# A recurrent attention stage with its output rows by transposes, an earlier first decay part, gate strips on GpSimd and VectorE, and a third decay part masked after the exponential

## The reference, cut to what matters

```
log_D  = (cs[s] - cs[t] + ig[t])  for t <= s, else -inf      # per sequence and head, 256 x 256
D_mat  = exp(log_D - max_t log_D)
C      = (q @ k.T / sqrt(32)) * D_mat
C_norm = C / (max(|sum_t C|, exp(-max_log_D)) + eps)
h      = layernorm(C_norm @ v) * (1 + ln_w)                  # over a head's 32 features
y      = (a * sigmoid(g)) @ w2[e] + b2[e]                    # expert e of the token
out    = x + h * silu(y)
```

## Time and profile before

| | |
|---|---|
| median of 3 runs | 233.12 us (232.3 to 234.32) |
| the profiled execution | 232.86 us, of it 231.0 us span |
| PE busy | 211.4 us, 92% |
| DVE busy | 173.7 us, 75% |
| ACT busy | 135.4 us, 59% |
| POOL busy | 107.5 us, 47% |

### The profile page before, as it was taken

One profiled execution on the slowest core, in us unless ns is written; L12 is line 12 of the kernel. 1 busy time (PEld: TensorE's weight loads), 2 busy tenths in 40 slices (PEclk: granted clock), 3 DMA queues, 4 the chain that ended last, 5 costly groups with the idle time before them and its releaser, 6 DMA issues.

```text
span 231.0 us, 6117 instructions
## 1 busy us (share of the span) xinstructions
PE 211.4 (92%) x1847; PEld 173.8 (75%) x1856; DVE 173.7 (75%) x490; ACT 135.4 (59%) x309; POOL 107.5 (47%) x140
## 2 busy tenths in 40 slices
PE   7998989889999999999999999999999999999430
PEld 6887745546555555699999999999999999986110
DVE  5998699975776767587679888988798878570590
ACT  2388757897887977655555555556556555520220
POOL 7667920077777771003333354336443643474250
PEclk9999999999999999999999999999999999999995
DMA  6999999998111115110790211220211000000993
GB/s 166 326 396 414 310 254 249 250 256 223 52 60 49 57 55 127 31 25 25 211 271 14 61 26 54 54 70 6 66 45 34 25 14 29 23 23 14 297 315 103
DMA packets 29761, 29.32 MB, mean 127 GB/s; under 512 B 3319, under 2 KB 24831, under 8 KB 29729
## 3 DMA queue, kind: packets, MB, share of 16 engines
q1 hardware_dynamic: 25138, 20.46, 28.9%
q0 software_dynamic: 3424, 8.38, 14.7%
q10 hardware_dynamic: 1168, 0.10, 0.4%
HBM read 20.01 MB, written 9.38 MB: 127 GB/s over the span
## 4 chain that ended last, share of the span: by engine, by line
PE 74%; DVE 10%; issue 5%; DMA 4%; ACT 1%; POOL 1%; SPq 1%; DVEq 0%; POOLq 0%; ACTq 0%
PE bank L1213 15%; PE head_bank L1213 15%; PE bank L1222 14%; PE head_bank L1169 6%; PE bank L1181 5%; PE bank L1156 5%; PE bank L1198 4%; PE bank L1155 3%; DVE stats L703 3%; PE bank L1095 2%; DMA xw<-y_tokens 2%; PE head_bank L1136 2%; DMA x_sb<-in_L_attn_x 1%; PE head_bank L1064 1%; DVE mv L709 1%
## 5 line engine op out<-in xcount | busy, mean ns | idle before, releaser
L458 POOL DMA_INDIRECT y_tokens<-ffn,idx x39 | 39.4, 1010 | 74.7 <-DVE ffn L1002 74.1
L452 POOL DMA_INDIRECT xs_sorted<-xw,pos x32 | 31.2, 975 | 25.8 <-DVE pos L849 16.4
L1222 PE MATMUL bank<-w_sb,dm 128*128 x312 | 41.3, 275 | 0.5 <-DVE dm L986 0.5
L1213 PE MATMUL bank<-xsT,wc 128*128 128x128 f32 x320 | 39.5, 276 | 0.3 <-DVE wc L869 0.3
L1222 PEld LDWEIGHTS bank<-w_sb,dm 128*128 128x128 f32 x312 | 38.0, 192 | 0.7 <-issue 0.7
L1213 PEld LDWEIGHTS bank<-xsT,wc 128*128 128x128 f32 x320 | 37.5, 192 | 0.7 <-DVE wc L869 0.5
L1213 PE MATMUL head_bank<-xsT,wc 128*128 128x128 f32 x304 | 37.0, 275 | 0.0
L877 DVE TENSOR_TENSOR cm<-dm,head_bank 128x1024 f32<-128x1024 f32 (+1 forms) x32 | 29.1, 950 | 9.6 <-PE head_bank L1169 6.5
L1213 PEld LDWEIGHTS head_bank<-xsT,wc 128*128 128x128 f32 x304 | 35.4, 192 | 0.0
L605 ACT ACTIVATE wc<-w_sb 128x512 f32 x39 | 24.6, 630 | 15.1 <-issue 15.0
L591 ACT ACTIVATE dm<-bank 128x512 f32<-128x512 f32 x48 | 26.9, 595 | 5.9 <-PE bank L1156 4.9
(11 more groups left out here) (199 smaller groups left out, 360.2 us busy)
## 6 DMA issues: line engine op xcount, KB each, us to landing
x_sb<-in_L_attn_x SPq DMA_DIRECT2D x16, 256.0 KB, 5.0
w_sb<-in_L_ffn_w SPq DMA_DIRECT2D x8, 512.0 KB, 8.3
w_sb<-negated_rows POOLq DMA_DIRECT2D x8, 508.0 KB
xs_sb<-xs_sorted SPq DMA_DIRECT2D x13, 193.5 KB, 2.6
xs_sorted<-b_sb SPq DMA_DIRECT2D x1, 2048.0 KB, 13.0
xw<-y_tokens SPq DMA_DIRECT2D x8, 256.0 KB, 4.8
out_x<-xw SPq DMA_DIRECT2D x8, 256.0 KB, 3.4
y_tokens<-ffn,idx POOLq DMA_INDIRECT x39, 2.3
```

Source lines behind the costliest of these rows:

```text
L452: pool.indirect_dma_start(xs_dram, bass.IndirectOffsetOnAxis(ap=pos[:, t:t + 1], axis=0), xw[:, t, :], None).then_inc(s_scat, 16)
L458: pool.indirect_dma_start(y_dram, bass.IndirectOffsetOnAxis(ap=idx[:, j:j + 1], axis=0), ys_sb[:, j // CH % 2, j % CH, :], None, bounds_ch ...
L1213: last = pe.matmul(bank[2 * (j % 2) + k][:, c * P:(c + 1) * P], wc[:, j % 3, m:m + P], xsT[:, j % 2, :], start=True, stop=True)
L1222: last = pe.matmul(bank[6 + j % 2][:, 0:D], uT[:, j % 2, c, :], w2_sb[:, bass.ds(e * (HC * D) + c * D, D)], start=(c == 0), stop=(c == HC ...
```

## The change

1. **Token rows.** `token_rows` uses two transposes in place of the two matmuls with `spread`. The ones move to column 0 of each head in `u_all`, the 31 values to columns 1 to 31; column 32 gets the sum of the 31, by a new reduction `last_columns` on VectorE for two sequences at once (turns b = 3, 5, ..., 15, and once after the loop). It is the last feature with the wrong sign, and `gamma` is negated there. `outputs` goes from VectorE to ScalarE, 256 columns.
2. **First decay part earlier.** TensorE: `scores(b+1)`, `log_decay(b+2, 0)`, `values_sum(b)`, `log_decay(b+2, 1)`, `log_decay(b+2, 2)`, `token_rows(b)`. ScalarE: `decay(b+2, 0)`, `evac_u(b)`, `decay(b+2, 1)`, `decay(b+2, 2)`, `outputs(b)`.
3. **Strips.** The twelve right strips of j = 1 to 3 are made by GpSimd, one after the other, after its weight DMAs and before the indirect DMAs. `left_rows` goes to VectorE, in turn b for b+3.
4. **Third part.** `log_decay(b, 2)` has no mask matmul. After the exponential, `masked(b)` on VectorE takes the minimum of `dm` part 2 and `keep` (3e38 or 0), 128 x 512, in place; it runs in turn b-1 after `weigh(b-1)`, for b = 0 between the two parts of `weigh(0)`.

```diff
@@ gpsimd
-            pool.tensor_copy(spread[:, :, 0:DH - 1], idh[:, :, 0:DH - 1]).then_inc(s_spread, 1)
...
+            pool.memset(keep[:, :], BIG).then_inc(s_keep, 1)
...
+            pool.affine_select(out=keep[:, :], in_=keep[:, :], compare_op=ALU.is_ge, fill=0.0,
+                               base=0, pattern=[[1, P]], channel_multiplier=-1).then_inc(s_keep, 1)
...
+            pool.tensor_scalar(last_of_head, last_of_head, -1.0, None, ALU.mult).then_inc(s_gamma, 1)
...
+            pool.wait_ge(s_ind, 4)
+            pool.wait_ge(s_sel, 2)
+            pool.wait_ge(s_seld, 1)
+            for j in range(1, NBS):
+                for h in range(NH):
+                    pool.tensor_scalar(right[:, h, j, :], sel[:, j, :], rmask[:, 0, h:h + 1], rmask[:, 1, h:h + 1],
+                                       ALU.mult, ALU.add).then_inc(s_rtp, 1)
@@ scalar
-            def left_rows(b):
...
+            def outputs(b):
+                act.wait_ge(s_o, b + 1)
...
+                act.activation(u_all[:, 2 * b:2 * b + 2, :, 0:DH],
+                               bank[7][:, 0:2 * D].rearrange("p (k h d) -> p k h d", k=2, h=NH), ACT.Copy).then_inc(s_oe, 1)
...
             for b in range(2):
                 for m in range(3):
                     decay(b, m)
-                left_rows(2 + b)
             for b in range(B):
                 if b == B - 1:
                     act.wait_ge(s_cm, 2 * (B - 1))
                     gate(0)
+                if b + 2 < B:
+                    decay(b + 2, 0)
                 evac_u(b)
                 if b + 2 < B:
-                    for m in range(3):
-                        decay(b + 2, m)
+                    decay(b + 2, 1)
+                    decay(b + 2, 2)
+                outputs(b)
...
-                    right_rows(b // 4 + 1, 2 * (b % 4))
-                    right_rows(b // 4 + 1, 2 * (b % 4) + 1)
-                if b + 4 < B:
-                    left_rows(b + 4)
@@ vector
+            def masked(b):
+                dve.wait_ge(s_keep, 2)
+                dve.wait_ge(s_dm, 3 * b + 3)
+                tail = dm[:, b % 2, :, 2, :]
+                dve.tensor_tensor(tail, tail, keep[:, :].unsqueeze(1).to_broadcast([P, NH, P]), ALU.min).then_inc(s_mk, 1)
...
+            def last_columns(b):
+                dve.wait_ge(s_oe, b + 2)
+                rows = u_all[:, 2 * b:2 * b + 4, :, :]
+                dve.tensor_reduce(rows[:, :, :, DH], rows[:, :, :, 1:DH], AX.X, ALU.add).then_inc(s_lc, 1)
...
+                left_rows(2)
                 for b in range(B):
                     weigh(b)
                     if b == 0:
                         evac_q(NQA + 1)
-                    if b >= 1:
-                        outputs(b - 1)
+                    if b == 0:
+                        dve.wait_ge(s_sel, 2)
+                        dve.wait_ge(s_seld, 1)
+                    if b + 1 < B:
+                        masked(b + 1)
+                    if b + 3 < B:
+                        left_rows(b + 3)
+                    if b >= 3 and b % 2:
+                        last_columns(b - 3)
@@ tensor
-                if m != 1:
+                if m == 0:
                     pe.matmul(bank[n % 2][:, :], ident_bf[:, :], maskn[:, :, :].rearrange("p h t -> p (h t)"), start=True, stop=False)
...
-                    last = pe.matmul(bank[7][:, k * n:(k + 1) * n], uTs[:, k * P:(k + 1) * P],
-                                     spread[:, :, :].rearrange("p h d -> p (h d)"), start=True, stop=True)
+                    last = pe.transpose(bank[7][:, k * P:(k + 1) * P], uTs[:, k * P:(k + 1) * P], ident[:, :])
...
+                if b + 2 < B:
+                    log_decay(b + 2, 0)
                 values_sum(b)
                 if b + 2 < B:
-                    log_decay(b + 2, 0)
                     log_decay(b + 2, 1)
+                    log_decay(b + 2, 2)
...
                 token_rows(b)
-                if b + 2 < B:
-                    log_decay(b + 2, 2)
```

More of the change, by code:

```diff
@@ L101, in mlstm_moe_block @@
         center = sb("center", [P, NH, DH])
-        spread = sb("spread", [P, NH, DA])
         triones = sb("triones", [P, S])
         maskn = sb("maskn", [P, NH, P], BF16)
+        keep = sb("keep", [P, P])
         desc8 = sb("desc8", [P, E])
@@ L300, in mlstm_moe_block @@
         s_maskc = sem("s_maskc")
-        s_spread = sem("s_spread")
+        s_lc = sem("s_lc")
+        s_keep = sem("s_keep")
+        s_mk = sem("s_mk")
+        s_rtp = sem("s_rtp")
         s_uones = sem("s_uones")
@@ L875, in weigh, with left_rows @@
                 for m0, m1 in ((0, 2), (2, 3)):
-                    dve.wait_ge(s_dm, 3 * b + m1)
+                    if m1 == 2:
+                        dve.wait_ge(s_dm, 3 * b + m1)
+                    else:
+                        if b == 0:
+                            masked(0)
+                        dve.wait_ge(s_mk, b + 1)
                     dve.tensor_tensor(cm[:, b % 2, :, m0:m1, :], dm[:, b % 2, :, m0:m1, :],
                                       head_bank[:, :, m0 * P:m1 * P].rearrange("p h (m t) -> p h m t", t=P), ALU.mult).then_inc(s_cm, 1)
-            def outputs(b):
-                dve.wait_ge(s_o, b + 1)
-                if b == FORGET:
-                    dve.tensor_copy(tm[:, :, :], bank[7][:, 3 * P:3 * P + 2 * R].rearrange("p (k r) -> p k r", k=2)).then_inc(s_tm, 1)
-                dve.tensor_copy(u_all[:, 2 * b:2 * b + 2, :, :].rearrange("p k h d -> p (k h d)"),
-                                bank[7][:, 0:2 * NH * DA]).then_inc(s_oe, 1)
+            def left_rows(b):
+                if b >= 4:
+                    dve.wait_ge(s_ld, 3 * (b - 3))
+                dve.tensor_scalar(left[:, b % 4, :], sel[:, b // 4, :], lmask[:, 0, b % 4:b % 4 + 1],
+                                  lmask[:, 1, b % 4:b % 4 + 1], ALU.mult, ALU.add).then_inc(s_lf, 1)
+            def last_columns(b):
+                dve.wait_ge(s_oe, b + 2)
+                rows = u_all[:, 2 * b:2 * b + 4, :, :]
+                dve.tensor_reduce(rows[:, :, :, DH], rows[:, :, :, 1:DH], AX.X, ALU.add).then_inc(s_lc, 1)
             def attention():
@@ L909, in attention @@
                 product(0)
-                outputs(B - 1)
+                last_columns(B - 2)
             def normalise(g):
@@ L1152, in log_decay @@
                         pe.wait_ge(s_lf, b - 1)
[L1153 to L1154 removed]
+                    if j == 0:
+                        pe.wait_ge(s_rt, 2)
+                    else:
+                        pe.wait_ge(s_rtp, NH * j)
+                if m == 0:
                     pe.matmul(bank[n % 2][:, :], ident_bf[:, :], maskn[:, :, :].rearrange("p h t -> p (h t)"), start=True, stop=False)
                 pe.matmul(bank[n % 2][:, :], left[:, b % 4, s0:s0 + P], right[:, :, j, t0:t0 + P],
[L1157 removed]
+                          start=(m != 0), stop=True).then_inc(s_ld, 1)
             def scores(b):
```

39 lines of the change are left out of this document (15 added, 24 removed).

## The result

The changed kernel takes **240.31 us** (median; 239.9 to 242.23) where the kernel before took 232.75 beside it: ratio 1.0322, interval 1.0274 to 1.037. It is slower by 7.6 us; forecast were 240.5 us and 7.4 more. All that follows is read in the profiled execution of 239.9 us, whose span is 238.0, 7.0 over that of before.

The account below looks back on a forecast made before the run. TensorE looked like the bound before; after the change VectorE would decide the loop. Start 3.8, loop 2.6 and end 1.0 sum to 7.4 us on 232.86, 240.3, stated as 240.5; range 234.8 to 244.

Parts of the forecast that it names:

- The loop, +2.6: Eleven turns from scores(4) to scores(15), set by VectorE: 41.7 us against 39.1 before, 2.6 us slower.
- the rules: Loop: earliest starts of VectorE's minimum, `weigh` and the next scores in each turn; 7.4 to 7.6 us per pair of turns.
- The rival in which TensorE goes on deciding: Loop: turns of 3.1 us if the minimum costs 0.3 and not 0.6; total 230.0 us, chance 0.08.
- TensorE's turn, 3.1: Loop: TensorE's own work and waits in one turn sum to 3.1 us; alone, a gain of 0.4 us a turn.
- The start, +3.8: Up to scores(4): 56.7 us against 52.9, about 2.7 from the VectorE-GpSimd conflict and 1.1 from VectorE's longer queue.
- the conflict, priced at 2.7: Start: VectorE's small routing instructions each wait for one GpSimd strip, both reading SBUF; about 2.7 us.
- the rival without a conflict, at 0.22: Start: GpSimd's strips run beside VectorE's routing instructions; scores(4) only 1.1 us later, total 237.8 us, chance 0.22.
- The worse start: Start: strips of 0.75 us or more and TensorE falling to half clock; total 243 to 244 us, chance 0.12.
- The end, +1.0: Loop's end: ScalarE's outputs 14 and 15 each put about 0.5 us before an expert block; 1.0 us slower.
- The total, 240.5: Whole kernel: 7.4 us more than the profiled 232.86 is 240.3; stated as 240.5 us, with chance 0.45.
- It cancels: Whole kernel: loop turns of 3.35 us pay for the slower start; about 232.8 us, chance 0.13.
- The scatters: Indirect DMAs start at about 52 instead of 46.6 us, yet stay hidden behind the loop with 2 us to spare.

Follow-up runs that it names:

- its second profile: The changed kernel run again with nothing changed, beside the kernel before at 233.47 us: 241.3 us, ratio 1.0328.
- the kernel with three mends: Changed kernel with third part masked on TensorE, GpSimd's strips behind the six routing instructions, sorted rows copied before the last two outputs: 232.43 us, ratio 0.9977.
- the fastest one: The kernel with three mends, plus all positions in VectorE's turn 0 and eight of GpSimd's twelve strips moved to VectorE: 227.92 us, ratio 0.9786.

## Why the prediction was right, point by point

**The loop, +2.6: measured +2.5.** Both the rule and its pattern hold: 3.14 and about 4.5 us by turns, 7.64 for the pair quoted above where the rules gave 7.4 to 7.6, because the minimum, which waits for the third exponential, begins at S + 3.81 (79.34 less 75.53) and not S + 3.65. VectorE's work of 0.6 + 0.27 + 0.6 in an odd turn fits as well. The wait at the head of its queue was in the rules, though nobody priced it there: the minimum at S + 3.65 and the end of `weigh` at S + 1.06 + 1.82 are 0.77 us apart, and the trace has 0.92, and 5.7 in all. What I did not see is that this wait is the term on which the turn hangs. The rival in which TensorE goes on deciding was tied to the minimum's price ("0.3 and not 0.6"). That price was right, 0.69 busy and 0.61 from start to start, but with a price of 0.3 the rules still put `weigh` of an odd turn at S + 3.65 + 0.3 + 0.27 + 0.6 = S + 4.82, behind the S + 4.16 at which its scores let it go (3.1 + 1.06). The condition was the place: the moved minimum costs the same, and turns are 3.28. For the same reason my expectation for the moved minimum was too long.

**TensorE's turn, 3.1: measured 3.13 to 3.14**, in even turns, where VectorE is not late. The single terms are less right than the sum: the mask matmul, priced at 0.22 with 0.15 of wait for `uTs` in return, so at 0.07 net, is worth 0.03.

**The start, +3.8: measured +3.2.** S1 comes 1.0 us earlier than forecast, and all of it is the links: done at 41.2 and not at 42.2. A strip was priced at 0.6 and takes 0.55 (7.04 for the twelve, forecast 7.2), and a link gets one strip in its way, but only five of six do, each 0.32 to 0.33 us longer: 1.6 us, and 0.2 for the `left` strip behind them (0.57 for 0.34). So the conflict, priced at 2.7, is worth 1.8 where it happens. The strips behind the links give back 1.4 us in the median against 240.31 (1.6 by the ratios, whose intervals overlap) and 1.8 to 3.0 at S3, the half clock's share included. Without that share it is less: the kernel with TensorE kept at work has the conflict, the one with the strips later has not, and both have the whole clock. They are 1.7 us apart from S0 to S1 (6.78 and 5.06) and 1.05 from S0 to S3 (14.22 and 13.17), since the later strips cost something in the turns behind. The sum of +3.8 is nearer than its parts: the conflict was 0.9 too dear, and the half clock, 0.4 us of this profile at S4 against the kernel with TensorE kept at work (18.47 and 18.03 from S0 to S4), was not in it.

The Trainium skill, SBUF — State Buffer, section "SBUF: two separate sides", has the loser of the exclusive lock blocked for the whole instruction of the other. This case's runs agree, both ways round: a link takes 0.49 beside strips of 0.55 and 0.17 without them, and the strip beside the minimum of 0.68 takes 1.10. By the records that strip begins 0.08 us ahead of the minimum (42.77 and 42.85) and is still the one that is lengthened; which of the two had the ports first no run shows. `weigh`, which reads one of its inputs from PSUM, keeps its 1.21 us beside strips (41.22 in the kernel with the strips behind the links). So the rival without a conflict, at 0.22, is out: the links did not keep their 0.17.

**The worse start**, a rival at 0.12, came in part: the clock was half after a pause of 3.16 us, but the strips were not dearer, and where the forecast had up to 3.1 us for the clock, half of it hidden, it cost 0.7 to 2.0 at S3. The Trainium skill, TensorE: Matmul & The Clock Gate, section "The HAM clock gate", has a paused engine fall back to half rate; the profile agrees (0.50 at 46.0 to 48.5), and so does its absence where TensorE was kept at work.

**The end, +1.0: measured +1.3**, 1.1 to 1.2 of it undone by the order of ScalarE alone. From S15 to the second expert block it is 7.97 us in the changed kernel and 6.68 before (98.63 less 91.95), so the whole 1.3 lies there.

**The total, 240.5: measured 240.31.** That it is this close is luck in part: the start was 0.6 us too dear, the end 0.3 too cheap, and the medians are 0.6 us further apart (7.6) than the two profiled spans (7.0). The rival "It cancels" was wrongly summed: eleven turns of 3.35 us gain 2.2, and with +3.8 and +1.0 that gives 235.4; its 232.8 needs a start of +1.1.

**The scatters, hidden "with 2 us to spare": right in one of two profiles.** In the first profile of the changed kernel the reads begin at 94.29 and take some 2.7 us as in the other kernels, and TensorE comes for the rows at 99.32: 2.3 us to spare. In its second profile it waits 0.48 us: reads begin 4.2 us after the last indirect DMA has started (95.22, 99.41) and not 2.3 (91.98, 94.29), as also in the two runs with the strips behind the links and the sorted rows first (4.4). Nothing of the total hung on this, but every mend did: the rows took 2.14, 2.29 and 3.65 us back, and the clock after them.

**What stays open.** Why the half clock lasted 3.4 us in one profile of the changed kernel and 6.8 in the next; how the 4.5 us between the kernel with three mends and the fastest one divide between earlier positions and fewer strips ahead of the DMAs; and why the last indirect DMA landed 2 us later in some profiles.

## What to carry to other kernels

An instruction that waits for another engine belongs at the end of its turn in an in-order queue: here a turn with the same VectorE work took 0.5 us less with the waiting minimum last. Before a loop is shortened, price what is hidden behind it: 32 indirect DMAs at 1.27 us were free at 39 us of loop and the bound at 35, and only with their positions earlier and fewer strips ahead of them did the loop's gain turn into time. Small dependent instructions of VectorE don't go beside GpSimd's back-to-back work on SBUF: five of six links here waited for one instruction of GpSimd each.

## What the runs showed of the hardware that was not expected

- A chip on which engines stand still for up to 8.08 us with "issue" as the releaser, the kernel before included (245.23 us against 232.7 to 233.5 on others).
- The granted clock fell to half at different times around the same pause of TensorE: in one execution at 44.5 us, with TensorE at rest from 42.6 to 45.8, in the other at 45.9, 1.5 us after a pause of 3.16 us had ended. `scores(1)` took 1.67 us in the one and 0.94 in the other.
- A wait of 3.65 us ahead of the expert stage cost another 1.14 us in the block behind it (3.16 against 2.02).
- A strip of GpSimd takes 0.55 us alone and 1.10 beside a VectorE instruction of 0.68 with both inputs in SBUF.
